# Edge sums by feature quarters, turned in 32x32 blocks on VectorE, and counts added from a 16-bit SBUF copy

## What is computed

```python
h = relu(layernorm(x))
# layer 0
msg = (h[src] + edge_attr_512) @ Wm.T + bm
agg = segment_sum(msg, dst) / max(deg, 1)
out = h + gelu(concat(h, agg) @ Wu.T + bu)
x = x + layernorm(out) * gamma + beta
# layer 1
h = relu(layernorm(x))
rst = (1 + eps) * h + segment_sum(h[src], dst)
x = x + (relu(rst @ W1 + b1) @ W2 + b2 + h)
```

## Time and profile before

| | |
|---|---|
| median of three runs | 526.91 us (526.67 to 529.15) |
| the profiled execution | 526.39 us, span 524.6 us |
| PE busy | 482.8 us, 92% of the span |
| VectorE busy | 283.0 us, 54% |
| GpSimd busy | 166.8 us, 32% |
| ScalarE busy | 147.5 us, 28% |
| granted TensorE clock, mean | 0.99 |
| edge loads | 78 of 1 MB, median 7.6 us from issue to landing |

### The profile page before, as it was taken

How to read it: one execution, slowest core, us unless ns; L and a number is a source line. 1 busy time by engine, 2 the same in 40 slices (tenths; PEclk the granted TensorE clock), 3 DMA queues, 4 the chain that set the end, 5 groups by cost and what they waited for, 6 DMA issues and landing times.

```text
span 524.6 us, 8826 instructions
## 1 busy us (share of the span) xinstructions
PE 482.8 (92%) x3003; PEld 277.0 (53%) x3003; DVE 283.0 (54%) x660; ACT 147.5 (28%) x291; POOL 166.8 (32%) x217
## 2 busy tenths in 40 slices
PE   5889999898898988999999999599989999999997
PEld 4446554444444544675665655379944446744442
DVE  6897887888777779645434789983000000011111
ACT  4416644123222223222237245441011122100000
POOL 7323665333322224000023267636994000000000
PEclk9999999999999999999999999799999999999999
DMA  8998998889999999988820111112040000011111
GB/s 299 316 367 301 338 327 292 348 342 361 352 367 358 374 363 390 408 308 315 271 82 2 32 29 41 35 62 100 1 163 0 0 0 1 0 41 40 41 40 35
DMA packets 31115, 98.95 MB, mean 189 GB/s; under 512 B 3577, under 2 KB 3577, under 8 KB 31067
## 3 DMA queue, kind: packets, MB, share of 16 engines
q1 hardware_dynamic: 30458, 97.27, 50.7%
q10 hardware_dynamic: 608, 1.05, 0.7%
HBM read 95.76 MB, written 2.56 MB: 187 GB/s over the span
## 4 chain that ended last, share of the span: by engine, by line
PE 63%; DVE 21%; issue 6%; PEld 6%; DVEq 1%; POOL 1%; DMA 1%; SPq 0%; PEldq 0%; POOLq 0%
PE ps L1260 13%; PE ps L1245 13%; PE ps L1007 9%; PE ps L1048 7%; DVE A L669 5%; PE ps L1105 5%; PE ps L1106 4%; PE ps L1018 4%; PE ps L1194 3%; PEld ps L1171 3%; PE ps L1036 3%; PEld ps L1172 2%; DVE U L893 2%; DVE tt L871 2%; DVE oneS L648 2%
## 5 line engine op out<-in xcount | busy, mean ns | idle before, releaser
L400 POOL TENSOR_TENSOR aggT<-turned_sums,aggT 128x88 f32 x118 | 53.9, 456 | 107.4 <-ACT turned_sums L473 94.4
L1007 PE MATMUL ps<-ea,oneD 128*22 128x256 f32 x1264 | 83.9, 383 | 1.4 <-DVE oneD L640 0.9
L947 DVE TENSOR_TENSOR U<-ps,U 128x512 f32<-128x512 f32 (+1 forms) x10 | 6.9, 692 | 130.8 <-PE ps L1260 130.8
L467 ACT COPY packed_sums<-ps 128x256 f32<-128x256 f32 x79 | 29.4, 372 | 163.9 <-PE ps L1007 163.9
L1245 PE MATMUL ps<-aggT,W1s 128*128 (+1 forms) x192 | 67.4, 513 | 2.2 <-PEq L1239 2.2
L1260 PE MATMUL ps<-W2s,hid 128*128 128x512 f32 (+1 forms) x160 | 68.8, 592 | 0.0
L669 DVE TENSOR_TENSOR A<-ps,A 128x220 f32 x158 | 60.3, 381 | 8.6 <-PE ps L1018 8.0
L1018 PE MATMUL ps<-oneK,oneS 128*128 128x220 bf16 x316 | 42.5, 259 | 14.7 <-DVE oneS L648 13.0
L1245 PEld LDWEIGHTS ps<-aggT,W1s 128*128 128x128 f32 x192 | 36.4, 190 | 33.1 <-issue 33.0
L1007 PEld LDWEIGHTS ps<-ea,oneD 128*22 128x22 f32 x1264 | 30.5, 101 | 41.1 <-issue 23.6
L648 DVE TENSOR_TENSOR oneK<-iotaP,P_key 128x880 bf16<-128x880 bf16 x79 | 51.8, 655 | 0.0
(11 more groups left out here) (139 smaller groups left out, 645.1 us busy)
## 6 DMA issues: line engine op xcount, KB each, us to landing
ea<-in_edge_attr_dram SPq DMA_DIRECT2D x78, 1024.0 KB, 7.6
X<-in_x_dram SPq DMA_DIRECT2D x1, 2304.0 KB
xt<-in_x_dram SPq DMA_DIRECT2D x9, 256.0 KB, 2.7
out_dram<-U SPq DMA_DIRECT2D x9, 256.0 KB
W1s<-in_L_gnn_W_dram SPq DMA_DIRECT2D x1, 2048.0 KB, 7.7
W2s<-in_L_gnn_W_dram SPq DMA_DIRECT2D x1, 2048.0 KB, 8.7
WuN<-in_L_gnn_Wu_dram ACTq DMA_DIRECT2D x1, 1024.0 KB, 5.4
WuN<-in_L_gnn_Wu_dram SPq DMA_DIRECT2D x1, 1024.0 KB, 6.8
```

The lines of the kernel that those rows point to most:

```text
L400: nc.gpsimd.tensor_tensor(cols, sums, cols, ALU.add).then_inc(early_step, 1)
L1007: last = T.matmul(to.rearrange("p (c d) -> p c d", c=2), oneD[h][:, g * 2 + j, :], data, start=j == 0, stop=j == 1)
```

## The change

- **Edge sums.** `sums(n)` now gives each quarter of PSUM a quarter (32) of every 128-feature chunk, and puts the two halves of the group side by side. That makes 16 calls of 128 columns for a group where there were 8 of 256; each call is two instructions, since the data are fp32. In this layout a transpose of each 32x32 block by itself gives feature by node as `aggT` wants it. So VectorE's block transpose (`turn`) writes `turned_sums` straight from PSUM. `packed_copy`, `turned_copy` and PE's transposes are gone. GpSimd (groups below 59) and VectorE (the others) both add from `turned_sums` in SBUF.
- **Waits.** PE's `sums(n)` waits for the transpose of group n - 2 where it waited for ScalarE's copy. The transpose waits for its sums and for the adds of group n - 2.
- **Counts.** ScalarE copies 128 x 440 counts from PSUM to `counted`, 16-bit (`counts_copy`). VectorE adds from there. PE's counts wait for the copy of batch m - 2.
- **Order on VectorE.** An iteration begins with the transpose of group n - 1, and the edge one-hot is made there for group n + 2, waiting for the sums of group n - 1. It has three slots (`SUM_HOTS`).
- **Small things.** The degree products on PE have a place of their own (`degree_products`), and `stats2` is gone in favour of `stats`.

```diff
-                for j in range(2):
-                    for g in range(2):
-                        for q in range(2):
-                            rows = (q * 2 + g) * QUAD
-                            data = ea[s][:, g * 2 + j, :].rearrange("p (c q d) -> p q c d", c=2, q=2)[:, q]
-                            to = ps[rows:rows + W, n % 2, 0:256]
-                            last = T.matmul(to.rearrange("p (c d) -> p c d", c=2), oneD[h][:, g * 2 + j, :], data,
-                                            start=j == 0, stop=j == 1)
+                for g in range(2):
+                    for j in range(2):
+                        data = ea[s][:, g * 2 + j, :].rearrange("p (k q e) -> p q k e", k=FC, q=FC)
+                        for q in range(FC):
+                            last = T.matmul(ps[q * QUAD:q * QUAD + W, n % 2, g * P:(g + 1) * P].rearrange("p (k e) -> p k e", k=FC), oneD[h][:, g * 2 + j, :],
+                                            data[:, q], start=j == 0, stop=j == 1)
...
+            def turn(n):
+                dve.wait_ge(sums_done, n + 1)
+                if HOTS <= n < HOTS + EARLY:
+                    dve.wait_ge(early_step, (n - HOTS + 1) * 2)
+                elif n >= HOTS:
+                    dve.wait_ge(sum_step, (n - HOTS + 1 - EARLY) * 2)
+                V.transpose(turned_sums[n % HOTS][:], ps[:, n % 2, 0:D // 2]).then_inc(turned, 1)
...
+            def counts_copy(m):
+                act.wait_ge(counts_done, m + 1)
+                if m >= HOTS:
+                    act.wait_ge(add_step, (m - HOTS + 1) * 2)
+                nc.scalar.copy(counted[m % HOTS][:], ps[:, 4 + m % 2, 0:2 * KW]).then_inc(counts_out, 1)
...
-                V.tensor_tensor(cols, ps[:, 4 + m % 2, half * KW:(half + 1) * KW].rearrange("p (h w) -> p h w", w=W), cols, ALU.add).then_inc(add_step, 1)
+                V.tensor_tensor(cols, counted[m % HOTS][:, half * KW:(half + 1) * KW].rearrange("p (h w) -> p h w", w=W), cols, ALU.add).then_inc(add_step, 1)
...
-                if n + HOTS < NG:
-                    sums_hots(n + HOTS)
+                if n > 0:
+                    turn(n - 1)
                 if n > EARLY:
                     sum_first = offsets(n - 1)
+                if n > 0 and n - 1 + SUM_HOTS < NG:
+                    sums_hots(n - 1 + SUM_HOTS)
```

More of the change, by code:

```diff
@@ L18 @@
 HOTS = 2
+SUM_HOTS = 3
 W = 22
@@ L109, in gnn_kernel @@
     ea = [place(f"ea{s}", [P, SUB, D], F32)[0] for s in range(SLOTS)]
-    oneD = [place(f"oneD{s}", [P, SUB, W], F32)[0] for s in range(HOTS)]
+    oneD = [place(f"oneD{s}", [P, SUB, W], F32)[0] for s in range(SUM_HOTS)]
     oneS = [place(f"oneS{s}", [P, 2, P, 2], BF16)[0] for s in range(HOTS)]
@@ L113, in gnn_kernel @@
     turned_sums = [place(f"turned_sums{s}", [P, D // 2], F32)[0] for s in range(HOTS)]
-    packed_sums = [place(f"packed_sums{s}", [P, D // 2], F32)[0] for s in range(HOTS)]
+    counted = [place(f"counted{s}", [P, 2 * KW], U16)[0] for s in range(HOTS)]
     at[0] = -(-at[0] // 64) * 64
@@ L163, in gnn_kernel @@
     mv, _ = place("mv", [P, NT, 2], F32)
-    stats2, _ = place("stats2", [P, NT, 6], F32)
     mv2, _ = place("mv2", [P, NT, 2], F32)
@@ L395, in add_sums_of @@
                     if half == 0:
-                        pool.wait_ge(turned_out, n + 1)
+                        pool.wait_ge(turned, n + 1)
                     if n > 0 or half > 0:
                         pool.wait_ge(early_step, n * 2 + half)
-                    sums = turned_sums[n % HOTS][:].rearrange("p (f q) -> p f q", f=FC)[:, :, half * QUAD:half * QUAD + W]
+                    sums = turned_sums[n % HOTS][:].rearrange("p (h k w) -> p h k w", h=2, w=QUAD)[:, half, :, 0:W]
                     nc.gpsimd.tensor_tensor(cols, sums, cols, ALU.add).then_inc(early_step, 1)
@@ L518, in _ @@
                         transposed_h0(k)
+                for m in COUNTS[n]:
+                    counts_copy(m)
                 for b in range(NT):
@@ L636, in sums_hots @@
             def sums_hots(n):
[L637 to L638 removed]
+                if n >= SUM_HOTS:
+                    dve.wait_ge(sums_done, n - SUM_HOTS + 1)
                 n1 = idxT["srel"][:, :, n:n + 1].broadcast_to([P, SUB, W])
[L640 removed]
+                V.tensor_tensor(oneD[n % SUM_HOTS][:], iotaF[:, 0:W].rearrange("p (a n) -> p a n", a=1).broadcast_to([P, SUB, W]), n1,
                                 ALU.is_equal).then_inc(hotD_ready, 1)
@@ L678, in add_sums_of @@
                     dve.wait_ge(sum_step, (n - EARLY) * 2 + half)
-                sums = ps[:, 2 + n % 2, 0:256].rearrange("p (f q) -> p f q", f=FC)[:, :, half * QUAD:half * QUAD + W]
+                sums = turned_sums[n % HOTS][:].rearrange("p (h k w) -> p h k w", h=2, w=QUAD)[:, half, :, 0:W]
                 V.tensor_tensor(cols, sums, cols, ALU.add).then_inc(sum_step, 1)
@@ L727, in _ @@
                 source_hots(n)
+            sums_hots(HOTS)
             dve.wait_ge(x_in, 32)
@@ L1020, in counts, with degree_products @@
                 last.then_inc(counts_done, 1)
-            def turn(n):
-                pe.wait_ge(packed_out, n + 1)
-                if 2 <= n < EARLY + 2:
-                    pe.wait_ge(turned_out, n - 1)
-                elif n >= EARLY + 2:
-                    pe.wait_ge(sum_step, (n - 1 - EARLY) * 2)
-                if n == DEG_AT + 1:
-                    pe.wait_ge(deg_step, 2)
-                if n == DEG_AT - 1:
-                    pe.wait_ge(fold_step, HB)
-                    T.transpose(ps[0:1, DEG_BANK, 256:256 + P], most[:], ident[:])
-                    for d in range(NT):
-                        T.matmul(ps[:, DEG_BANK, 384 + d:385 + d], Dsum[:, d * P:(d + 1) * P], onesF[:, 0:1], start=True, stop=True)
-                for c in range(2):
-                    last = T.transpose(ps[:, 2 + n % 2, c * P:(c + 1) * P], packed_sums[n % HOTS][:, c * P:(c + 1) * P], ident[:])
-                last.then_inc(turned, 1)
+            def degree_products():
+                pe.wait_ge(fold_step, HB)
+                T.transpose(ps[0:1, DEG_BANK, 256:256 + P], most[:], ident[:])
+                for d in range(NT):
+                    last = T.matmul(ps[:, DEG_BANK, 384 + d:385 + d], Dsum[:, d * P:(d + 1) * P], onesF[:, 0:1], start=True, stop=True)
+                last.then_inc(deg_mm, 1)
             def transpose_h0(b):
@@ L1103, in piece @@
                     to = bank("D", f, cols) if q == 2 else ps[:, 4 + f, 0:cols]
-                    counted = (ARd if q == 2 else ARc)[:, c, :]
-                    T.matmul(to, Hh[:, c, rows], counted, start=c == 0 and (q < 2 or f % 2 == 0), stop=False)
-                    last = T.matmul(to, Hl[:, c, rows], counted, start=False, stop=c == NT - 1 and (q < 2 or f % 2 == 1))
+                    here = (ARd if q == 2 else ARc)[:, c, :]
+                    T.matmul(to, Hh[:, c, rows], here, start=c == 0 and (q < 2 or f % 2 == 0), stop=False)
+                    last = T.matmul(to, Hl[:, c, rows], here, start=False, stop=c == NT - 1 and (q < 2 or f % 2 == 1))
                 last.then_inc(piece_mm, 1)
```

47 lines of the change are left out of this document (16 added, 31 removed).

## The result

The changed kernel takes 542.92 us (median of 4 runs, 541.53 to 543.41), the kernel before 527.22 us beside it. The ratio is 1.029, 95% interval 1.025 to 1.032: it is slower by 15.7 us, where 528.5 was forecast. The time lies inside the range (513 to 544), but 14 us from the point, where the range reaches for the sake of rivals 2 and 3. The profiled execution took 541.53 us, span 539.7.

A forecast was written before the change was run, and what follows sets the result against it. Bound: stage A (groups 2 to 59, counting) by VectorE's work plus its losses behind U products; stage B (groups 60 to 78) by PE. Stage A +6.4 and stage B -4.6 gave 528.5 us, range 513 to 544.

The forecast's parts named there:

- Rival 2: Counting stage: each GpSimd add meets a VectorE operation, costing 15 us in place of 8; 538 us, chance 0.14.
- Rival 3: VectorE: adds at 22-element runs stay at the slow rate (+18) or a transpose takes 0.60 us (+14); 543 us, chance 0.13.
- The adds (-18.2 us): Groups 2 to 59: 152 VectorE count adds fall from 0.30 to 0.18 us each, saving 18.2 us.
- The transposes (+20.9 us): Groups 2 to 59: VectorE gains 58 transposes of 0.36 us each, 20.9 us added.
- The port (+8 us): Groups 2 to 59: VectorE operations with both inputs in SBUF are delayed by GpSimd, 8 us added, bounds 0 and 15.
- The idle time behind a U product (-5.3 us): Groups 2 to 59: VectorE idles 2.2 us in place of 2.73 behind each of ten U products, 5.3 us saved.
- The idle time elsewhere: Groups 2 to 59: no term; the stage was taken as VectorE's work plus what it loses behind each U product.
- ScalarE (+1 us): Groups 2 to 17: other ScalarE copies stand ahead of the counts' copy, 1 us added, bounds 0 to 3.
- Stage B (-4.6 us): Groups 60 to 78, no counting, PE alone sets the pace: transposes leave PE, 19 x 0.24 = 4.6 us saved.
- Rival 1: Counting stage: transposes and GpSimd's adds fall mostly into VectorE's idle time behind U products; 515 us, chance 0.23.
- Rival 4: PE's sums cost by the matmul, not the column, so 32 take 2.0 us; 562 us, chance 0.05.
- The signs: Right: groups 2 to 59 take 170 to 180 us, VectorE over 88% busy; groups 60 to 78 take 2.95 to 3.0 each.

The follow-up runs named there:

- `banks_onek`: Changed kernel with three PSUM banks for the edge sums in place of two, and VectorE's order oneK, add, oneS, add (both repairs): 525.1 us, ratio 0.995.

## Why the prediction was right or wrong

- **The adds (-18.2 us).** Right within 3 us: 0.19 to 0.20 us from start to start against 0.18, so 15 to 17 us. Rival 3 is out: the 22-element runs are not at the slow rate (it had 0.30), nor does a transpose take 0.60.
- **The transposes (+20.9 us).** Right: 0.37 us against 0.36, 21.5 us.
- **The port (+8 us).** Too large. VectorE's busy time rose by 8.5 us. With the measured prices the adds and the transposes give 5 to 6 of that, which leaves 2 to 4 us for the port and the rest. Without GpSimd's adds VectorE is busy 10.3 us less, of what the forecast had at some 5 as paid before and 7 as new. (Its sum of today's delays, 79 x 0.16, is 12.6 and not 12.8 us, which changes nothing.) Rival 2 gave 538 us by the port deciding; taking all of GpSimd's adds away leaves 536.4, so it does not decide. The Trainium skill ("SBUF — State Buffer", SBUF: two separate sides) gives the port pair to the one that starts first, for its whole instruction, and blocks the other. The trace agrees. The kind of operation fits: count adds from SBUF are held up, the transposes out of PSUM are not (median 0.44 us with GpSimd's adds and without). The size fits too: a held-up add ends 0.12 to 0.16 us behind GpSimd's instruction. The prediction set the rule aside because it took a blocked instruction to lose the whole length of the other, 0.34 us; it loses what is left of it when it comes, for most held-up adds some 0.15 us.
- **The idle time behind a U product (-5.3 us).** The new size is about right: the ten waits of the count add behind a U product are 1.32 to 3.45 us, 23.9 us together, 2.4 each against 2.2. The old size was not. The 2.73 us of the earlier trace rows are one place; over all ten the kernel before idles 24.8 us (1.0 to 3.3 each) and not 27.3. So 0.9 us were saved and not 5.3, a miss of 4.4.
- **The idle time elsewhere: this step failed.** The sum had VectorE's work plus what it loses behind the ten U products. That nearly held for the kernel before: 24.8 of 28.4 us, and most of the rest stands at the start of the stage. In the changed kernel 16.5 us of idle time stand elsewhere where 3.6 did, which is 12.9 us for which the forecast had nothing. Nearly all of it is in the twenty further waits for the copy. All in all, idle time went up by 12.0 us instead of down by 5.3, a miss of 17.3 (4.4 and 12.9), less 2.2 us by which VectorE was less busy than forecast and ScalarE's 1 us: the 14 us. The prediction named both new waits, "PE's sums of group n now wait for VectorE's transpose of group n-2", and the copy's 0.6 us, and named what is queued behind the add (oneK, and the next transpose). But it let them work once per U product. It did not ask whether the loop that they close fits into an iteration between the U products. With one batch it doesn't: 2.93 us from a transpose to the add that follows from it, against 2.45 of VectorE's own work. It also gave no thought to what PE's new waits do to the clock: PE stood still before its sums, six half-clock stretches came with that, and 8.5 us of the further waits lie there. The runs price the two waits: 8.3 us for the sums' wait, 9.6 us for oneK behind the copy, 17.8 together, and with both repaired stage A is 168.8 us.
- **ScalarE (+1 us).** No run separates it. ScalarE is busy 57 of 189 us.
- **Stage B (-4.6 us).** Right as a sum (4.3), not in its parts. A group saves 0.14 to 0.15 us and not 0.24, 19 x 0.15 = 2.8: the first product stays stretched, as the rows of the changed kernel below show, 0.33 us from start to start. The other 1.5 us come from one group (70), which fell from 4.77 to 3.31 us. There VectorE moves a finished aggregation bank, for which PE waits; before, this stood behind the edge one-hot's wait for the sums of that group, and the new order has no such wait. The forecast did not see that.

```profile
249.87 1.07 PE L1010 MATMUL ps<-ea,oneD 128*22 128x128 f32 x32
250.88 0.50 PE L1098 MATMUL ps<-ARc,Hh 128*128 128x512 f32 x1
251.21 0.40 PE L1099 MATMUL ps<-ARc,Hl 128*128 128x512 f32 x1
...
252.93 1.07 PE L1010 MATMUL ps<-ea,oneD 128*22 128x128 f32 x32
```

- **Rival 1 (515 us).** Wrong for this kernel: idle time grew by 12 us where the rival had it shrink by 9. With both repairs idle falls to 16 us and the time moves that way, to 525.
- **Rival 4 (562 us, by the matmul).** Out: 32 matmuls take 1.01 us (249.87 to 250.88), as 16 did. The 62 ns a matmul that the Trainium skill ("TensorE: Matmul & The Clock Gate", Wait — 56ns, not 53.3ns?) names for one mode of decoding are not the price here: the trace shows 32 ns for each.
- **The signs.** Slower had the highest chance, 0.43, but it was carried by the port and by the prices. The mechanism that made it slower had no rival of its own, and the range holds 542.9 us by luck: rivals 2 and 3 widened it for reasons that the runs rule out. The signs say so. Stage A was to be 170 to 180 us with VectorE over 88% busy, and is 189 us with 79%; a group of stage B was to be 2.95 to 3.0 us, and is 3.07. None of the signs of being wrong had a stage A above 180 us.

## What to carry to other kernels

When a change puts a new engine or a new wait into a loop between two engines, add up the whole way round (here transpose, sums, counts, copy, add) and compare it with the time that the busiest engine needs for the same stretch. A loop that is longer hands delays round between the rare long instructions too, and does not only lose time behind them. Look also at what the bottleneck's new waits do to TensorE's clock. A latency costs little where the instruction that waits for it stands behind work that doesn't: moving one instruction past the wait was worth 10 to 13 us here and nothing in the kernel without the copy. And a step may go to different engines in different stages, to whichever has room there.

## What the runs showed of the hardware

- The granted TensorE clock, 1.00 through all of stage A before, fell to 0.50 in six stretches of the changed kernel, each of which starts with or just behind a wait of 1.1 to 2.3 us before PE's sums. Not every such wait brought one: those of 1.70 us before the sums at 115.01 and 184.71 did not. At 0.50 the sums take 1.92 us for 1.07. With fewer waits (`banks_onek`) one group with such long sums was left; with filler matmuls four groups were left whose sums took over 1.2 us.
- A 32x32 block transpose of 128 x 256 fp32 from PSUM to SBUF takes 0.44 us on VectorE, 0.37 from start to start, with no share in what GpSimd's adds cost: its median is 0.44 with them and without.
- A 16-bit add of VectorE with both inputs in SBUF can be held up until a GpSimd instruction beside it ends: the adds of stage A lie at 0.26 to 0.30 us where they meet none, and the 49 that are held up (most at 0.39 to 0.49 us, up to 1.10 beside a subtraction of 1.28 us) all end 0.12 to 0.16 us behind GpSimd's instruction.
- An add of 220 16-bit elements in runs of 22, at an offset from a register, takes 0.19 to 0.20 us from start to start on VectorE, where the fp32 add from PSUM took 0.30.
